# Attention biases folded into lifted rows, expert scatters taken out of the first loops, weights split in the setup

## The reference

```python
xn = layernorm(x)                                   # no gain, no bias
# block A, for each of the 4 batches of 2048 rows
Q, K, V = (layer_norm(xn @ W + b, g, c) for W, b, g, c in (q, k, v))
phiQ, phiK = tanh(Q @ Wphi_q + bphi_q) + 1, tanh(K @ Wphi_k + bphi_k) + 1   # K, V have a row of zeros in front
alpha = softmax(mean(Q) . K) * L                    # a weight for each row and head
attn = (phiQ @ (phiK * alpha)^T V) / (phiQ @ sum(phiK * alpha) + eps)
attn = layer_norm(attn + gamma * (conv5(attn) + conv_b), lna_g, lna_b)
s = attn + gelu(attn @ W1 + b1) @ W2 + b2 + xn
# block B: attention over the 4 sequences at one position, a projection, then
# a router that sends each row to 2 of 16 experts (1280 places each)
h = xn + attention(layernorm(xn)) @ proj
g = silu(h + experts(layernorm(h)))
out = x + s * g
```

## Time and profile before

| | |
|---|---|
| median of 3 runs | 2003.02 us (2002.83 to 2003.76) |
| the profiled execution | 2004.66 us, its span 2002.9 us |
| PE busy | 1805.4 us (90%) |
| DVE busy | 1370.3 us (68%) |
| POOL busy | 1064.7 us (53%) |
| ACT busy | 814.7 us (41%) |

### The profile page before, as it was taken

One profiled execution on the slowest core, in us unless ns is written; L12 is line 12 of the kernel. 1 busy time (PEld: TensorE's weight loads), 2 busy tenths in 40 slices (PEclk: granted clock), 3 DMA queues, 4 the chain that ended last, 5 costly groups with the idle time before them and its releaser, 6 DMA issues. The chain is left out here.

```text
span 2002.9 us, 37020 instructions
## 1 busy us (share of the span) xinstructions
PE 1805.4 (90%) x12775; PEld 1616.6 (81%) x12776; DVE 1370.3 (68%) x3444; ACT 814.7 (41%) x1946; POOL 1064.7 (53%) x1499
## 2 busy tenths in 40 slices
PE   3899996398998999997999999999969899999998
PEld 2676775285898867996999999999956799885998
DVE  3988884754555545555878888887746577684676
ACT  1566663273323553232333333333346234472332
POOL 3666552675555565553678787787643133340431
PEclk9999997598999998998999999999989999998999
DMA  7555522123222122122455555644334011240110
GB/s 207 158 179 178 169 93 81 48 74 122 73 71 82 63 93 79 62 67 88 105 102 120 106 133 102 125 103 80 54 92 127 22 39 43 80 135 24 33 48 30
DMA packets 175285, 184.74 MB, mean 92 GB/s; under 512 B 25107, under 2 KB 166719, under 8 KB 175118
## 3 DMA queue, kind: packets, MB, share of 16 engines
q1 hardware_dynamic: 136990, 133.05, 21.9%
q0 software_dynamic: 33824, 49.51, 11.4%
q10 hardware_dynamic: 4304, 0.02, 0.1%
HBM read 98.16 MB, written 90.44 MB: 94 GB/s over the span
## 5 line engine op out<-in xcount | busy, mean ns | idle before, releaser
L1863 POOL DMA_INDIRECT after_d<-h,home x160 | 259.3, 1621 | 107.4 <-DVE h L1914 62.7
L1783 ACT ACTIVATE hid<-bank 128x512 f32<-128x512 f32 x160 | 95.7, 598 | 335.8 <-PE bank L129 335.8
L127 PE MATMUL bank<-rows_hi,up_hi 128*128 128x256 f32 x640 | 188.8, 295 | 12.9 <-DVE rows_lo L1907 8.1
L129 PE MATMUL bank<-rows_hi,up_lo 128*128 128x256 f32 x640 | 181.8, 284 | 0.0
L128 PE MATMUL bank<-rows_lo,up_hi 128*128 128x256 f32 x640 | 181.8, 284 | 0.0
L127 PE MATMUL bank<-down_hi,hid_hi 128*128 128x256 f32 x640 | 181.1, 283 | 0.0
L128 PE MATMUL bank<-down_lo,hid_hi 128*128 128x256 f32 x640 | 181.1, 283 | 0.0
L129 PE MATMUL bank<-down_hi,hid_lo 128*128 128x256 f32 x640 | 181.0, 283 | 0.0
L1202 POOL DMA_INDIRECT buf_d<-rows_in,to_row x128 | 134.8, 1053 | 86.5 <-POOL rows_in L1198 42.4
L1184 POOL TENSOR_SCALAR cnorm<-cmv 128x1 f32<-128x1 f32 x64 | 15.3, 239 | 278.7 <-DVE cmv L1695 277.7
L1930 DVE TENSOR_TENSOR hid_lo<-hid,hid_hi 128x512 fp32r<-128x512 f32 x160 | 132.6, 843 | 39.8 <-ACT hid_hi L1783 37.2
(11 more groups left out here) (321 smaller groups left out, 5566.4 us busy)
## 6 DMA issues: line engine op xcount, KB each, us to landing
buf_d<-zeros SPq DMA_DIRECT2D x16, 1360.0 KB, 7.4
rows_in<-buf_d SPq DMA_DIRECT2D x80, 272.0 KB, 3.2
rows_in<-ln_d SPq DMA_DIRECT2D x128, 128.0 KB, 2.1
x<-in_x SPq DMA_DIRECT2D x16, 512.0 KB, 4.1
after_d<-after SPq DMA_DIRECT2D x16, 512.0 KB, 2.9
ln_d<-ln SPq DMA_DIRECT2D x16, 512.0 KB, 2.9
xa<-in_x SPq DMA_DIRECT2D x16, 512.0 KB, 4.3
up_w<-in_w_t POOLq DMA_DIRECT2D x16, 512.0 KB, 4.1
```

What stands on the lines that cost most here:

```text
L127: pe.matmul(dst, hi, mhi, start=start and i == 0, stop=False)
L129: mm = pe.matmul(dst, lo, mhi, start=False, stop=end)
L1783: act.activation(dst[:, 2 * half:2 * half + 2].rearrange("p f c -> p (f c)"), bank[half][:], ACT.Gelu_apprx_tanh).then_inc(e_hid, 1)
L1863: pool.indirect_dma_start(after_d, bass.IndirectOffsetOnAxis(home[i % TAG_RING][:, r:r + 1], axis=0), h2[p][:, r], None, bounds_check=T - ...
```

## The change

The row biases are no longer added by products of their own. A normalised row has the mean zero, so a row that is lifted by one has the column sums of a weight added to its product. The weight is therefore changed once, in the setup, to `w + (bias - column sum) / 256`, and the rows are lifted by one where their bias `-mean/deviation` is made. The products with `one_rows` go away for q, k and v, for phiK and for the down product; the one of the convolution stays. POOL gets one more operation on 128 x 4 numbers for each group of x (16 times in all), one on 128 x 1 numbers for each tile (64 times), and one on 128 x 256 numbers for each tile in the second loop (64 times), the sum of `xnb` and `out_row`.

The scatter jobs of `attend(0)` stand at other places: none in the first loops, 16 in each middle, 16 in each second loop (at its first four tiles too).

The work on the weights leaves the routing block. In the setup now: the two passes over x of turn 0 (`xn`, `xn1`), six loads of rows that are spread over all partitions, the sums for the lifted weights on PE, the lifting on DVE, `wa_s` (ACT and DVE), `w2_s` (ACT and DVE), `wphi` for q (POOL). In the turns 1 and 2 of the front block: `w1` scaled and its high part (ACT), its low part and `b1c` (DVE), `wconv` (POOL). The loads of the first x groups of block A are issued in turn 16 of the front block and not behind its last turn.

```diff
@@ open_roots, norm_x
-            step = Chain(pool, ax_norm, b * 4 * GROUPS)
+            step = Chain(pool, ax_norm, b * 5 * GROUPS)
...
+            step(pool.tensor_scalar(xnorm[0][:, 1], xnorm[0][:, 1], 1.0, None, ALU.add))
@@ setup, SP
-                        load(brow[:, i * E:(i + 1) * E], row(a[name]), small_in)
-                    for i, name in enumerate(("bphi_k", "conv_b", "lna_b", "b2")):
-                        load(extra[:, i * E:(i + 1) * E], row(a[name]), small_in)
+                        load(qkv_row[:, i * E:(i + 1) * E], row(a[name]).to_broadcast((P, E)), small_in)
+                    load(brow[:], row(a["conv_b"]), small_in)
+                    for dst, name in ((phik_row, "bphi_k"), (out_row, "lna_b"), (b2_row, "b2")):
+                        load(dst[:], row(a[name]).to_broadcast((P, E)), small_in)
@@ setup, ACT
+                    act.wait_ge(x_norm, X_NORM)
+                    for k in range(S):
+                        act.activation(xn[0][:, k], x[0][:, k], ACT.Identity,
+                                       bias=norm[0][:, 1, k:k + 1], scale=norm[0][:, 0, k:k + 1]).then_inc(xn_made, 1)
...
+                    act.wait_ge(setup_step, LIFTED)
+                    act.activation(wa_s[0][:], wa[:], ACT.Copy).then_inc(wa_high, 1)
+                    act.wait_ge(loaded, 16 * LOADS)
+                    act.activation(w2_s[0][:], w2, ACT.Copy).then_inc(act_step, 1)
@@ setup, PE
+                    pe.wait_ge(wa_in, 16 * WA_LOADS)
+                    for j in range(HALVES):
+                        pe.matmul(bank[4][:], ones_f[:], wa[:, j, 0:2 * E], start=j == 0, stop=j == 1)
+                    for j in range(HALVES):
+                        last = pe.matmul(bank[5][:, 0:E], ones_f[:], wa[:, j, 2 * E:3 * E], start=j == 0, stop=j == 1)
@@ setup, DVE
+                    dve.wait_ge(sums_made, 4)
+                    step(dve.tensor_tensor(qkv_row[:, 0:2 * E], qkv_row[:, 0:2 * E], bank[4][:], ALU.subtract))
+                    step(dve.tensor_tensor(qkv_row[:, 2 * E:3 * E], qkv_row[:, 2 * E:3 * E], bank[5][:, 0:E], ALU.subtract))
+                    for j in range(HALVES):
+                        step(dve.scalar_tensor_tensor(wa[:, j], qkv_row[:], 1.0 / E, wa[:, j], ALU.mult, ALU.add))
...
+                    dve.wait_ge(wa_high, 1)
+                    dve.tensor_tensor(wa_s[1][:], wa[:], wa_s[0][:], ALU.subtract).then_inc(wa_high, 1)
+                    dve.wait_ge(act_step, 1)
+                    dve.tensor_tensor(w2_s[1][:], w2, w2_s[0][:], ALU.subtract).then_inc(wa_high, 1)
@@ front block, SP
+                        if is_turn(t, BT):
+                            for g in range(2):
+                                open_load(sp, 0, g)
@@ front block, POOL
+                        if is_turn(t0, 2):
+                            step = Chain(pool, pool_step, MASK_STEPS + 2)
+                            pool.wait_ge(conv_in, 16 * H)
+                            step(pool.tensor_scalar(wconv[:], wconv[:], gamma[:, 0:1], None, ALU.mult))
+                            for j in range(HALVES):
+                                step(pool.tensor_tensor(wconv[:, j, 2], wconv[:, j, 2], ident[:], ALU.add))
@@ front block, ACT
+                        if is_turn(t0, 1):
+                            step = Chain(act, act_step, 1)
+                            for j in range(HALVES):
+                                step(act.activation(w1[:, j], w1[:, j], ACT.Copy, scale=lna[:, 0, j:j + 1]))
+                            step(act.activation(w1_s[0][:], w1[:], ACT.Copy))
@@ front block, DVE
+                        if is_turn(t0, 1):
+                            dve.wait_ge(sums_made, 5)
+                            dve.tensor_tensor(b1c[:], bank[6][:, 0:MLP // P], b1c[:], ALU.add).then_inc(wa_high, 1)
+                        if is_turn(t0, 2):
+                            dve.wait_ge(act_step, 4)
+                            dve.tensor_tensor(w1_s[1][:], w1[:], w1_s[0][:], ALU.subtract).then_inc(wa_high, 1)
@@ routing block: the work of POOL, the sums of PE for b1c and the splits of ACT are gone
@@ attend
-                soon = range(BT // 2) if scatters else range(BT)
-                amid = range(BT // 2, EACH - BT + 4) if scatters else ()
+                amid = range(EACH - BT) if scatters else ()
@@ attend, POOL
-            if scatters and i % 2 and i < BT:
-                                scatter(job_of(b, i // 2))
...
+                                step(pool.tensor_scalar(qnorm[k % 2][:, 1, 1:2], qnorm[k % 2][:, 1, 1:2], 1.0, None, ALU.add))
...
                             k = i - 3
                             if 0 <= k < BT:
+                                residual = Chain(pool, res_step, b * (3 * BT) + 3 * k)
+                                residual(pool.tensor_tensor(xnb[:, k], xnb[:, k], out_row[:], ALU.add))
                                 pool.wait_ge(c_mv, b * BT + k + 1)
...
-                            if scatters and 4 <= k < BT:
+                            if scatters and 0 <= k < BT:
                                 scatter(job_of(b, EACH - BT + k))
@@ attend, PE
-                                    pe.matmul(dst, one_rows[:], brow2[:, c:c + width], start=True, stop=False)
...
-                                pe.matmul(bank[PHIK_BANK][:, 0:E], one_rows[:], brow2[:, ROW_PHIK:ROW_PHIK + E], start=True, stop=False)
...
-                                    pe.matmul(dst, one_rows[:], brow2[:, ROW_OUT:ROW_OUT + E], start=True, stop=False)
```

175 lines of the change are left out of this document (86 added, 89 removed).

## The result

The changed kernel takes 2023.5 us (median of 4 runs, 2019.44 to 2026.24) where the kernel before, on the same chip, takes 2002.92 (1996.36 to 2003.76): ratio 1.0115, 95% interval 1.0093 to 1.0137. It is slower, by some 23 us; 2014 was forecast. The profiled execution took 2026.24 us with a span of 2024.5, 21.6 more than the span of before.

A forecast was written before the change was run, and what follows sets the result against it. PE (90% busy) was taken to set the pace in most loops, DVE the routing block, POOL a short stretch. Terms 2.3 + 7.5 - 4.8 - 12.1 - 28.1 + 22.2 + 17.5 + 6.6 gave +11.1: 2014 us, range 1995 to 2027.

The forecast's parts named there:

- Setup: Setup block: new loads, sums and lifting end it 6.5 us later, two ACT passes taken off give 4.2; sum +2.3.
- turns: Turns 1 and 2 of the front block: ACT's extra 4.2 us on the path plus 3.3 of DVE's subtraction; +7.5.
- end of front: End of the front block: x rows asked for a few turns earlier, ACT free for them at 338.5; -4.8 us.
- routing: Routing block: four DVE operations fall to 1.22 us each, 11.6 together, and `b1c` goes (0.45); -12.1.
- First loops: First loops: 32 steps save 0.45 us, 32 save 0.34 (-25.3); x roots +5.2, scatters gone -8; sum -28.1.
- Scatters in the middle: Middles of attend(0): sixteen jobs take about 62.2 us, delaying the first row norm; +11.1 per batch, +22.2.
- first tiles: Start of second loops: GpSimd's cycle becomes 7.4 us, +7.1 per batch of attend(0), +1.6 in attend(2); together +17.5.
- Pairs: Second loops: GpSimd's sum slows DVE's split, +0.27 us a pair in attend(0), +0.2 in attend(2); 28 pairs, +6.6.
- A: Rival: PE is the bound everywhere, first loops give -43.2, pairs -6.6; -17.2, 1986 us; chance 0.13.
- B: Rival: scatters in the middle never wait for a tile, sixteen take 52.8 us; 1995 us; chance 0.10.
- C: Rival: setup and turns 1 and 2 at their upper bounds, +9.2; 2023 us; chance 0.17.
- D: Rival: the first loops' pace stays at 4.09, since ACT's or DVE's list is longer; +20.1, 2034 us; chance 0.07.

The follow-up runs named there:

- Experiments 1: The kernel after with the scatters back at their old places, fold and setup kept: 1999.21 us, ratio 0.9998 to the kernel before.
- experiment 2: The kernel before with only the scatters moved to their new places, biases and setup unchanged: 2026.55 us, ratio 1.0117 to the kernel before.
- experiment 3: The kernel after without GpSimd's sum of tile and output row, so the result lacks that row: 2002.93 us, ratio 1.0021 to the kernel before.
- experiment 5: The kernel after with the loads of batch 1's first two x groups issued eight steps later: 2019.97 us, ratio 1.0102 to the kernel before.
- experiment 6: The kernel after with GpSimd's roots of an x group spread over two steps of the first loop: 2033.05 us, ratio 1.0162 to the kernel before.
- experiment 7: The kernel after with DVE's joins in attend(2)'s first loops 16 of 256 columns wide, output incomplete: 2013.11 us, ratio 1.0071 to the kernel before.
- 9: The kernel after with x roots over two steps and ACT's x row behind q, k and v: 2017.23 us, ratio 1.0079 to the kernel before.
- experiment 12: The kernel after with k's lift in DVE's copy, not a fifth GpSimd operation: 2014.89 us, ratio 1.0077 to the kernel before.
- experiment 8: Kernel after; scatters back, output row a PE product, k's lift in DVE's copy, attend(2)'s x roots over two steps: 1979.61 us, 0.9916 to before.
- 4: The kernel after with scatters at their old places and the output row added by a PE product again: 1991.1 us, ratio 0.995 to the kernel before.
- experiment 10: Kernel after; scatters back, output row a PE product, lift in DVE's copy, x roots split, ACT's x row last everywhere: 1986.12 us, 0.9923 to before.

## Why the prediction came out as it did

The direction was right and the time, 2023.5, lies in the range; the size was not, +11 against +20.6 by medians and +23 by ratio. Experiments 1 and 2 part the forecast in two. For the scatters it had -8 in the first loops, +22.2 in the middles and 11 of the first tiles, +25.2 in all; alone they measure +23.4. For the rest, the fold and the setup, it had -14.1; measured is 0. The miss is there.

**Setup, turns, end of front, routing: right in sum, two terms off.** +2.3 came out as -0.2 in the profiled run. The vectors were in at 17.75 (I took 18), but the sums over `wa` were done at 25.6 and not 28. In the seven experiments that share setup and front block with the kernel after (1, 3, 5, 6, 7, 9, 12) the first transposes start 1.2 to 2.9 us later than before, as forecast; the -0.2 is a lucky run. The turns cost 11.7 and not 7.5, by the last logits (338.21 before, 349.64 after, 11.4 later, less what the start gave): 9.7 of it is there at the first logits, the rest comes behind turns 1 and 2. In those seven runs the cost is 7.1 to 9.9. ACT's 4.2 is in it; how the remainder divides between DVE's work and the granted clock (0.50 from 50.7 to 64.3 us, and before only from 53.1 to 59.9) no run tells. The x rows of ACT follow the logits by 0.12 instead of 5.09, so -5.0 against -4.8. The routing stage, from DVE's first operation to the next block's first product, is 40.55 before and 28.36 after, -12.2 against -12.1.

**First loops: the step that failed.** "So 32 steps save 0.45 and 32 save 0.34: -25.3", with 5.2 for x and 8 of scatters. The pace itself was right: 3.62 for 3.64 in attend(0), and 3.61 and 3.81 in turn, 3.71 on average, for 3.75 in attend(2). The number of steps was not. Sixteen per batch were counted, and only the eleven from tile 4 on run at the pace of the earlier trace rows; the ones ahead run in the fill or at the pace of the second loop in which they lie (in batch 1 8.12 and 8.59 us before, 7.76 and 8.00 after). The mistake lies in how I read the earlier trace rows: "15 steps take 61.38 us, 4.09 each", "without a gap". The first four of these 15 steps take 4.81, 4.67, 3.10 and 4.22 us, and there is a gap in them:

```profile
1477.78 0.47 PE L1401 MATMUL bank<-brow,one_rows 128*128 128x512 f32 x1 [1.77 <-ACT qkn L1292]
```

That the mean of the four, 4.20, is near the steady step's 4.08 is chance.

Without the scatters' part (experiment 2 against before, -6.3 for the forecast's -8), the fold gave -11.6 in place of -20.1, and that divides so. The eleven steps of attend(0) gave 6.9 in both batches (experiment 2 against after), for 7.3. Those of attend(2) gave 3.2 for 4.9: DVE's joins held them, and with the joins cut (experiment 7) they gave 6.4. The 20 steps ahead of tile 4 had 7.9 of the -25.3 and gave 2.5, of which experiment 2 has 1.0 for the scatters: without those, 6.4 of the 8.5 that are missing are here. In part this may be the lower clock shown above for 391 to 396 us, which no experiment set by itself.

GpSimd's fifth operation, the lift, is not the miss: I had 0.3 for two steps, 9.6 over 64, and without it (experiment 12) the first loops are 5.4 to 9.0 us shorter. Only the places differ: nothing in a steady step of attend(0), 0.1 in one of attend(2), and more behind x roots.

**Interaction, not foreseen.** My terms were added as if independent. With the scatters in their old places the fold makes the first loops of attend(0) longer (160.1 against 154.7), for in their steps GpSimd's list is the bound, and the lift makes it longer (without it, experiment 8 against 4, they are 7.0 shorter); a list that is no bound once the scatters are moved is one while they stand there.

**Scatters in the middle, first tiles: right in mechanism and size.** Sixteen jobs took 62.0 us for 62.2 (446.75 to 508.77), the cycle is 7.38 for 7.4. The last job ended 14.7 us after the first `cmv`, not 11, since that `cmv` came 5.0 earlier in its middle under a granted clock of 1.00; the end of the first tiles does not depend on it. Batch 1's middle and first tiles together grew by 18.1 for 18.2; the agreement to 0.1 is chance, since among six kernels with the same lists there (after, 5, 6, 7, 9, 12) it is 18.1 to 20.0. Batch 0's grew by 22.2, 4.0 more than forecast. 2.7 of it is the 17th scatter's tile behind 1 MB of x (experiment 5). For the other 1.3 I have only the lower clock as a reason (0.75 over the first tiles of batch 0, 0.82 over those of batch 1), which no experiment tried by itself.

**Pairs: right for one pair, and the total in part by luck.** A steady pair is 0.29 us longer in attend(0) and 0.19 in attend(2), for 0.27 and 0.2, and both halves are measured (experiment 3). But from the fifth `cmv` to the 16th there are eleven tiles, 22 pairs in four batches and not 28, which is +5.2 at the forecast's sizes; and 2.5 of the +6.4 lie in the first distance of the two batches of attend(0), under the lower clock. By the rule of the Trainium skill that I had weighed against it (SBUF — State Buffer, Who interferes with whom), the sum would have cost the full 0.73 and the pairs +12; the runs are on the side of the row, with 0.52 and 0.42.

**The rivals.** A (PE bound everywhere) fell: the first loops gave 17.9 and not 43, and the pairs became longer. B fell: a job still waits for its tile, and sixteen took 62.0 us and not 52.8. C's time, 2023, is the measured one, but by luck and not by its cause: setup, front and routing together came out only 1.0 above the forecast. D fell: the pace is not 4.09.

## What to carry to other kernels

A saving per step counts only for the steps that the step's pace governs: count those between two steady marks, and price fill and overlap by themselves. An operation on an engine that is half idle can cost more than the product on the busiest one that it replaces, if another engine on the path works beside it (the sum: 0.42 to 0.52 us a pair, for rows worth 0.23), and one of 0.2 us is paid where it stands in the chain that links two steps. And when an operation is put later in a list, look at who is queued behind its readers: ACT's x row in experiment 6, SP's tile load in experiment 10. Before a difference of a stretch is laid to an edit, compare the granted clock of the two stretches.

## What the runs showed of the hardware

- The middles, which have the same products on PE in every kernel here, follow the granted clock of PE, over 56 middles in 14 profiles: 49.6 to 51.2 us at 1.00, 51.0 to 52.3 at 0.97, 52.4 to 53.9 at 0.94, 53.6 to 54.9 at 0.90 to 0.91. The same kernel gets one or the other: the two batches of the kernel after had 1.00 and 0.90.
- After a wait of 15.6 us PE was granted 0.50 of its clock for the next 4 us with 3.78 us of work in them, and 0.59 on average from 522 to 530 us, where its waits were 3.65 and less. The granted clock had fallen to 0.50 at 501.3, 4.8 us into the wait. That a stall costs more than its length is likely from this but not shown: the first tiles of batch 0 took 48.28 us and those of batch 1 39.87, but of these 8.4 us 3.7 is only an earlier first `cmv`, 2.7 the late tile, and 2.0 is left for the clock and all else.
- `TENSOR_TENSOR` of DVE, 256 columns, takes 0.43 us alone and 0.90 to 1.00 beside GpSimd's sums of 0.72 to 0.97, and the `CAST` of 256 columns 0.29 alone and 0.81 beside them.
- A scatter of two indirect DMAs holds GpSimd for 3.4 us even when its tile is there (0.18 tags, 0.81 wait, 1.1, 0.30, 0.98), and for 5.7 (407.41 to 413.10) when the tile's load stands in a queue behind another's wait (experiment 10).
- The runs of the kernel before lay between 1991.90 and 2004.21 us on one chip, and the experts' stretch, the same work in all, took 566.9 to 573.0 us in the profiled runs. A difference of one stretch by under 5 us between two profiles should be laid to an edit only with its rows beside it.
